# Attention scores contracted over 64 rows instead of 128, in an eight-sequence Macaron block on one core

## Reference

```
x = x + 0.5 * ffn(layernorm(x))
x = x + attention(layernorm(x))
x = x + 0.5 * ffn(layernorm(x))
ffn(h):       shared swiglu (hidden 256) + one of 8 experts per token (argmax of 8 logits,
              input scaled by the sigmoid of the largest logit, swiglu with hidden 256)
attention(h): 16 heads of width 8, rotary q and k, softmax(q k^T / sqrt(8)) v, then W_o;
              8 sequences of 256 tokens
```

## Time and profile before

| | |
|---|---|
| median of 3 runs | 401.68 us (401.1 to 401.76) |
| the profiled execution: its time | 405.68 us |
| its span, first to last instruction | 403.9 us |
| mean granted TensorE clock | 0.924 |
| busy: PE / weight load | 313.2 / 176.7 us |
| busy: DVE / ACT / POOL | 230.8 / 199.1 / 162.7 us |

### The profile page before, as it was taken

One profiled execution on the slowest core, in us unless ns is written; L12 is line 12 of the kernel. 1 busy time (PEld: TensorE's weight loads), 2 busy tenths in 40 slices (PEclk: granted clock), 3 DMA queues, 4 the chain that ended last, 5 costly groups with the idle time before them and its releaser, 6 DMA issues.

```text
span 403.9 us, 6408 instructions
## 1 busy us (share of the span) xinstructions
PE 313.2 (78%) x2104; PEld 176.7 (44%) x2104; DVE 230.8 (57%) x573; ACT 199.1 (49%) x451; POOL 162.7 (40%) x295
## 2 busy tenths in 40 slices
PE   1759749999246798989898989888874896699960
PEld 0125436666113444544454544444441363466640
DVE  8945312433176777878878787787834621243422
ACT  2108113544225568686868777876652531055520
POOL 3924730665347434342424332431221176035660
PEclk9999997999756699999999999999999798699995
DMA  7960134101210000000000000000000011501017
GB/s 219 169 270 20 54 105 79 42 39 41 96 40 1 2 1 2 2 0 2 2 1 2 2 0 2 3 1 2 2 0 2 0 52 52 153 20 47 39 41 214
DMA packets 24271, 18.37 MB, mean 45 GB/s; under 512 B 4944, under 2 KB 22608, under 8 KB 23984
## 3 DMA queue, kind: packets, MB, share of 16 engines
q1 hardware_dynamic: 21744, 12.84, 12.5%
q0 software_dynamic: 2496, 5.13, 3.5%
HBM read 10.26 MB, written 7.71 MB: 44 GB/s over the span
## 4 chain that ended last, share of the span: by engine, by line
DVE 30%; PE 27%; POOL 15%; issue 13%; another core or an unknown queue 7%; DMA 4%; ACT 2%; SPq 1%; POOLq 0%; DVEq 0%; ACTq 0%
PE bank L822 21%; DVE negmax L715 11%; POOL y_by_token L342 9%; DVE xn L579 5%; PE bank L974 3%; DVE sh L637 2%; DMA xs<-y_by_token 2%; DVE qT L708 2%; DVE rs L731 2%; DVE stats L589 1%; DMA y_by_token<-ys,xg 1%; POOL parts L374 1%; POOL parts L371 1%; POOL parts L373 1%
## 5 line engine op out<-in xcount | busy, mean ns | idle before, releaser
L715 DVE TENSOR_REDUCE negmax<-bank 128x2 f32<-128x512 f32 x128 | 82.1, 684 | 14.0 <-PE bank L822 13.6
L511 ACT ACTIVATE probs<-bank 128x512 f32<-128x512 f32 x128 | 72.1, 607 | 25.9 <-PE bank L822 25.4
L342 POOL DMA_INDIRECT y_by_token<-ys,xg x46 | 44.6, 970 | 57.6 <-DVE ys L683 30.0
L822 PE MATMUL bank<-kT,qT 128*128 128x512 bf16 x128 | 50.2, 393 | 10.6 <-DVE negmax L715 5.3
L822 PE MATMUL bank<-qT,kT 128*128 128x256 bf16 x256 | 48.9, 273 | 5.5 <-DVE qT L708 3.9
L822 PE MATMUL bank<-rgu,xgT 128*128 x92 | 48.8, 614 | 0.5 <-ACT xgT L481 0.5
L680 DVE TENSOR_TENSOR rh<-rsg,bank 128x256 f32<-128x256 f32 x46 | 19.4, 421 | 46.6 <-ACT rsg L489 46.6
L333 POOL DMA_INDIRECT xs_sorted<-xs,slot x32 | 31.5, 984 | 34.6 <-ACT xs L471 13.8
L519 ACT COPY kT<-bank 64x1024 bf16<-64x1024 bf16 x32 | 32.2, 1006 | 19.8 <-PE bank L974 19.6
L822 PE MATMUL bank<-probs,vx 128*32 128x256 f32 x512 | 39.0, 389 | 0.1
L489 ACT ACTIVATE rsg<-bank 128x256 f32<-128x256 f32 x46 | 17.6, 383 | 38.4 <-PE bank L822 38.4
(11 more groups left out here) (105 smaller groups left out, 488.8 us busy)
## 6 DMA issues: line engine op xcount, KB each, us to landing
xg<-xs_sorted SPq DMA_DIRECT2D x10, 258.0 KB, 4.7
rgu<-in_rgu SPq DMA_DIRECT2D x1, 2048.0 KB, 19.8
xs<-y_by_token SPq DMA_DIRECT2D x8, 256.0 KB, 3.5
xs_sorted<-xg SPq DMA_DIRECT2D x1, 1483.5 KB, 16.3
x<-in_x SPq DMA_DIRECT2D x4, 256.0 KB, 3.3
rdn<-in_rdn SPq DMA_DIRECT2D x1, 1024.0 KB, 16.3
out_x<-x SPq DMA_DIRECT2D x4, 256.0 KB, 2.6
y_by_token<-ys,xg POOLq DMA_INDIRECT x46
```

Of the source, the lines that this page charges most:

```text
L342: g.indirect_dma_start(y_dram, bass.IndirectOffsetOnAxis(ap=xg[:, j, D:ROW].bitcast(U32), axis=0), ys[:, j, :], None, bounds_check=N + SLO ...
L511: a.activation(probs[:, h % 8, :], stbank[st_bank(u, h)][:], ACT.Exp, scale=float(DH) ** -0.5).then_inc(exp_done, 1)
L715: v_.tensor_reduce(negmax[:, w, t, h0 + 2 * pair:h0 + 2 * pair + 2], sbank[k % 2][:].rearrange("p (a s) -> p a s", a=2), AX.X, ALU.max, ne ...
L822: return t_.matmul(o_, l, r, start=start, stop=stop, **k)
```

## The change

Keys are stored without zeros: `kT` has 8 blocks of 256 columns instead of 16, each with both heads of a pair, copied by one ACT instruction over 128 partitions. Each score matmul contracts only over its head's 64 partitions. `scores` of a step now covers one head and both query tiles, as two matmuls of 256 columns with two weight loads, instead of two heads and one query tile as one matmul of 512; `score_head` takes the odd head of a pair first, so that in a step `scores` and `scores_t` are on opposite 64 rows. `maxima` reads and writes by that order. POOL's memset of `kT` goes. The order of the steps and the other waits stay as they are.

```diff
...
         qT = [sb(f"qT{u}", [P, H // 2, L], BF16) for u in range(2)]
-        kT = [sb(f"kT{u}", [P, H // 2, 2, L], BF16) for u in range(2)]
+        kT = [sb(f"kT{u}", [P, H // 2, L], BF16) for u in range(2)]
         vstage = sb("vstage", [P, 2, 2, D], F32)
...
+        def score_head(k):
+            return 2 * (k // 2) + 1 - k % 2
...
             for u in range(2):
-                g.memset(kT[u][:].bitcast(F32), 0.0).then_inc(consts_set, 1)
                 g.memset(vx[u][:], 0.0).then_inc(consts_set, 1)
                 g.memset(parts[u][:].bitcast(F32), 0.0).then_inc(consts_set, 1)
-            pool.wait_ge(consts_set, 7)
+            pool.wait_ge(consts_set, 5)
             for u in range(2):
...
                     act.wait_ge(filled[name], i + 2)
-                    src = work[uses.index(name) % 2][:].bitcast(BF16).rearrange("p (r s) -> p r s", r=4)
-                    for k in range(2):
-                        ins = a.copy(kT[v][64 * k:64 * k + 64, 4 * half:4 * half + 4, k, :], src[64 * k:64 * k + 64])
-                    ins.then_inc(emptied[name], 1)
+                    a.copy(kT[v][:, 4 * half:4 * half + 4, :].rearrange("p r s -> p (r s)"),
+                           work[uses.index(name) % 2][:].bitcast(BF16)).then_inc(emptied[name], 1)
...
                     dve.wait_ge(s_filled, 8 * unit + k + 1)
-                    pair, t = k // 2, k % 2
-                    v_.tensor_reduce(negmax[:, w, t, h0 + 2 * pair:h0 + 2 * pair + 2], sbank[k % 2][:].rearrange("p (a s) -> p a s", a=2),
+                    v_.tensor_reduce(negmax[:, w, :, h0 + score_head(k)], sbank[k % 2][:].rearrange("p (t s) -> p t s", t=2),
                                      AX.X, ALU.max, negate=True).then_inc(s_reduced, 1)
...
-                    w, h0, unit = (u, 4, 2 * i + 1) if half == 0 else (v, 0, 2 * i + 2)
+                    w, h0, unit = (u, HH, 2 * i + 1) if half == 0 else (v, 0, 2 * i + 2)
                     if k == 0:
...
                         pe.wait_ge(s_reduced, 8 * unit + (k - 1))
-                    pair, t = k // 2, k % 2
-                    mm(sbank[k % 2][:], qT[w][:, h0 + pair, t * P:(t + 1) * P],
-                       kT[w][:, h0 + pair, :, :].rearrange("p a s -> p (a s)")).then_inc(s_filled, 1)
+                    h = h0 + score_head(k)
+                    rows = slice(64 * (h % 2), 64 * (h % 2) + 64)
+                    for t in range(2):
+                        ins = mm(sbank[k % 2][:, t * L:(t + 1) * L], qT[w][rows, h // 2, t * P:(t + 1) * P], kT[w][rows, h // 2, :])
+                    ins.then_inc(s_filled, 1)
...
                         pe.wait_ge(exp_done, 16 * i + (h - back + 1))
+                    rows = slice(64 * (h % 2), 64 * (h % 2) + 64)
                     for k in range(2):
-                        ins = mm(stbank[st_bank(u, h)][:, k * L:(k + 1) * L], kT[u][:, h // 2, h % 2, k * P:(k + 1) * P], qT[u][:, h // 2, :])
+                        ins = mm(stbank[st_bank(u, h)][:, k * L:(k + 1) * L], kT[u][rows, h // 2, k * P:(k + 1) * P], qT[u][rows, h // 2, :])
                     ins.then_inc(st_filled, 1)
```

## The result

The changed kernel takes 428.95 us (median of 4 runs, 426.02 to 430.75) against 401.5 before; the ratio is 1.068 with a 95% interval of 1.0615 to 1.074. The forecast was 399.0, its range 395.6 to 402.8. The profiled execution took 426.02 us, its span is 424.2, and its mean granted clock is 0.829 instead of 0.924. It was the fastest of the four, where the profiled execution before was 4.0 us above its median, so the difference between the two profiles understates that of the medians.

What follows compares the result with a forecast made beforehand. In attention DVE and PE alternate on the chain; near the start DVE is held by POOL's memsets. Terms of -3.31, -0.86, +1.44 and +0.09 gave -2.6 us, from the 401.7 median to 399.0, range 395.6 to 402.8.

Steps and rivals of the forecast that it cites:

- rival 5: Attention: fewer rows at work lower the granted clock, PE's part of each turn doubles, over 10 us in all; chance 0.03.
- The sum itself: Whole kernel: gains 3.31 and 0.86, losses 1.44 and 0.09, together -2.6 us; in general -4.9 + 38 x.
- The price of a change of partition: Attention chain: each of 38 steps between 128-row and 64-row work costs x, taken as 0.06 us, bounds 0 and 0.28.
- rival 3: Attention chain: a row step costs what a column step costs, 0.12 us; sum -0.3 us, 401.4 us; chance 0.14.
- Overlap: Scores on opposite row halves: first s starts with second t, saving 0.107 us at half 0's first step and after back.
- The memsets: Start of the kernel: without POOL's two kT memsets DVE finishes xn of chunk 3 earlier; gain 3.31 us, bounds 0 to 3.50.
- The 4.0 us between the profiled execution and the median: Whole kernel before: the median lay 4.0 us below the profiled execution; carried over, making 403.1 into 399.0 us.
- Key copies, maxima, second weight load: Attention: ACT saves 1.01 us per half off the chain, maxima reduce the same columns, the extra load is hidden; each 0.

Runs made afterwards that it cites:

- run with gaps alone: Kernel before, 128-row scores, one added 64-row, 32-column matmul ahead of each group of other work among scores, in five places: 406.54 us, ratio 1.011.
- filler run: Changed kernel plus four overwritten matmuls of 128 rows and 512 columns at the first scores_t of half 1: 416.89 us, ratio 1.037.
- run with fewer columns: Kernel before, 128 rows, each scores matmul cut to its first 256 of 512 columns, every second head's maxima stale: 396.62 us, ratio 0.981.

## Why the prediction was wrong

- *The step that failed* is rival 5, "fewer rows at work could lower the grant in attention", which got a chance of 0.03. I argued that in 300 to 310 us PE was busy only 5.30 of 10 us at the full grant, and that scores keep their columns. The first is a busy share of 128-row work, and so says nothing of 64-row work; before the change nothing else could be seen. In the changed kernel PE was busy 5.01 of 6.28 us ahead of a fall, no less than before (4.91), and still the clock fell, to 0.81 over attention. Attention grew by 29.3 us; by the prices below all but about 2 us of that is the clock (an estimate), the longer low stretch at its start included. The size in the rival, "over 10 us in all", was right as a bound; the chance was not. The sum itself had no term for the clock.
- *The price of a change of partition*, taken as 0.06, the middle between 0 and 0.12: 0.14 in the run with gaps alone and 0.14 in the filler run. At full clock the changed kernel shows it directly; the columns are start, duration and instruction:

```profile
187.37 0.39 PE L822 MATMUL bank<-kT,qT 64*128 64x256 bf16 x2
...
187.69 0.66 PE L1047 MATMUL bank<-tab,pvs 128*128 128x128 f32 x4
...
188.28 0.28 PE L822 MATMUL bank<-qT,kT 64*128 64x256 bf16 x1
...
188.29 0.28 PE L822 MATMUL bank<-kT,qT 64*128 64x256 bf16 x1
...
188.40 0.27 PE L822 MATMUL bank<-qT,kT 64*128 64x256 bf16 x1
188.41 0.27 PE L822 MATMUL bank<-kT,qT 64*128 64x256 bf16 x1
```

  Into the transposes 187.69 - 187.37 - 0.213 = 0.11, out of them 188.28 - 187.69 - 0.44 = 0.15. That is rival 3's price, 0.12, and a little more. The weight load of the transposes, which began 0.11 us ahead of them before (204.32 for 204.43), begins only with them here (187.69). The Trainium skill (TensorEngine Tiling (Array Packing), "Key Properties") says that a change of the tiling mode drains TensorE. The trace agrees by these gaps, and a change between the row halves shows none.
- *Overlap* exists and is larger than taken: where both heads' matmuls are queued, they start in pairs (188.28 and 188.29, 188.40 and 188.41), both from the first on, not only the second with the first. It gives about 0.4 us a turn, where the sum had 0.21, and the two changes around back eat 0.28 of it: a full-clock turn with half 0 over 64 rows is 0.1 us shorter.
- *The memsets*: place and mechanism right, 3.3 us in the profiled execution, a quarter to a half of it on average. The 4.0 us between the profiled execution and the median, carried over to the changed kernel, was one execution's too: there the profiled execution lay 2.9 us below the median.
- *Key copies, maxima, second weight load*: 0, as forecast. ACT's 16 us less of work moved nothing.
- Without the fall of the clock the sum, by these prices, would be -1 to -2 for the memsets, 38 x 0.14 = +5.3 for the changes and about -3 for overlap (eight turns of 0.4): about 1 us slower, an estimate, since no run had the whole changed kernel at full clock.
- Left open: every kernel with 64-row scores also had the gaps and the overlap, so rows without them weren't tried; gaps alone leave the clock up, and rows with gaps don't. Nor was 128-row work with half the columns tried.

## What to carry to other kernels

Before taking zeros out of a stationary and a moving operand, ask what they do for the clock: on a PE that is near full but has sparse stretches, half the rows can cost half the speed for a part of each turn, and the profile before can't show it, because busy time counts a 64-row matmul as a whole one. Mixing 64-row with 128-row work cost about 0.14 us per change on the chain. And price a memset on POOL beside DVE from several executions, since DVE may or may not get in between two of them.

## What the runs showed of the hardware that was not expected

- The granted clock went with the rows that the matmuls used, though half of them had only zeros in one operand: with the other 64 rows multiplying by zeros it stays at 2.4 GHz (0.99 in attention), without them it is 0.81. The Trainium skill (TensorE: Matmul & The Clock Gate, "What's actually happening") says that the clock is set by how busy the PE has been recently. By the profile's busy time that does not hold here: in the same 6.28 us of a turn PE was busy 4.91 us before and 4.49 in the run with fewer columns, and the clock stayed up; it was busy 5.01 in the changed kernel, and the clock fell.
- The same amount of 64-row work costs 0.5% in one half of the turn and 4.6% in the other.
- Adding 2048 columns of useless matmul per turn to the changed kernel made it 12 us faster; with 4096 the difference can't be told from none (1.060 against 1.068, with intervals that overlap).
- PE takes a 64-row matmul on one half while the other half is at work, at 0.01 us between starts.
